# Extra TensorE products of ones in the routing of a Macaron layer (MoE, Mamba, MoE)

## What is computed

```
x = x + 0.5 * moe(layernorm(x))
x = x + mamba(layernorm(x))
x = x + 0.5 * moe(layernorm(x))
```

```
logits = xf @ gate_w + gate_b                 # 4096 x 64 experts
top_l, top_i = top_k(logits, 3)
gates = softmax(top_l)
pos = (cumsum(onehot) * onehot).sum(-1) - 1   # place of each choice in its expert
valid = pos < 64
buf[e, pos] = xf[tok]                         # then two matrix products per expert with a GELU between
```

## Time and profile before

| | |
|---|---|
| Median of 3 runs | 862.25 us (859.62 to 864.14) |
| Profiled execution | 867.32 us, its span 865.6 us |
| TensorE busy | 683.7 us (79%) |
| VectorE busy | 623.0 us (72%) |
| GpSimd busy | 462.6 us (53%) |
| ScalarE busy | 419.1 us (48%) |
| Mean granted TensorE clock | 0.886 |

### The profile page before, as it was taken

How to read it: one execution, slowest core, us unless ns; L and a number is a source line. 1 busy time by engine, 2 the same in 40 slices (tenths; PEclk the granted TensorE clock), 3 DMA queues, 4 the chain that set the end, 5 groups by cost and what they waited for, 6 DMA issues and landing times. The chain is left out here.

```text
span 865.6 us, 27705 instructions
## 1 busy us (share of the span) xinstructions
PE 683.7 (79%) x11818; PEld 426.1 (49%) x11818; DVE 623.0 (72%) x1053; ACT 419.1 (48%) x779; POOL 462.6 (53%) x301
## 2 busy tenths in 40 slices
PE   5637999956456889899798989978886537999967
PEld 3625555545123445446454644545453525555546
DVE  7782555529246989899998989898996891555525
ACT  2410544420457867758676766756531320444520
POOL 3003666420013878798787778878992003566520
PEclk9857999979558999999999999989996757999979
DMA  8992999443055363443425353442004901999537
GB/s 289 396 322 74 341 378 300 160 153 153 5 167 182 120 201 103 140 153 111 154 92 183 111 155 137 114 153 97 3 4 158 396 29 47 329 379 308 181 112 295
DMA packets 92100, 155.47 MB, mean 180 GB/s; under 512 B 7315, under 2 KB 32541, under 8 KB 90704
## 3 DMA queue, kind: packets, MB, share of 16 engines
q1 hardware_dynamic: 87568, 141.40, 48.0%
q0 software_dynamic: 4416, 12.39, 4.1%
HBM read 112.02 MB, written 41.99 MB: 178 GB/s over the span
## 5 line engine op out<-in xcount | busy, mean ns | idle before, releaser
L1143 POOL TENSOR_TENSOR BIG<-BIG,R 128x1024 f32<-128x1024 f32 x128 | 301.1, 2372 | 65.5 <-DVE BIG L1097 65.4
L1097 DVE TENSOR_TENSOR_SCAN BIG<-BIG,ps 128x1024 f32<-128x1024 f32 x128 | 286.0, 2271 | 4.2 <-PE ps L849 2.9
L849 PE MATMUL ps<-BIG,stack 64*32 64x128 f32 x8192 | 154.1, 282 | 48.6 <-DVE BIG L1097 46.8
L849 PEld LDWEIGHTS ps<-BIG,stack 64*32 64x32 f32 x8192 | 118.9, 108 | 125.4 <-DVE BIG L1097 100.7
L1019 ACT ACTIVATE BIG<-BIG,An 128x510 f32<-128x510 f32 x192 | 124.0, 708 | 10.2 <-DVE BIG L1097 9.7
L717 POOL DMA_INDIRECT R<-xn_dram,tok_idx x64 | 65.2, 1019 | 100.7 <-DVE row_idx L645 80.9
L731 POOL DMA_INDIRECT y_dram<-BIG,row_idx x64 | 64.6, 1010 | 69.0 <-DVE BIG L669 63.3
L654 DVE COPY BIG<-ps 128x512 f32<-128x512 f32 x64 | 44.3, 692 | 74.1 <-PE ps L501 74.1
L390 ACT ACTIVATE BIG<-BIG 128x512 f32<-128x512 f32 x64 | 40.4, 631 | 104.9 <-DVE BIG L661 104.9
L871 PE MATMUL ps<-BIG,fold 128*32 128x512 f32 x512 | 70.1, 623 | 5.0 <-POOL BIG L1143 5.0
L501 PE MATMUL ps<-BIG 128*64 128x512 f32 x240 | 68.6, 651 | 0.0
(11 more groups left out here) (153 smaller groups left out, 972.4 us busy)
## 6 DMA issues: line engine op xcount, KB each, us to landing
BIG<-in_L_ffn_w SPq DMA_DIRECT2D x120, 512.0 KB, 6.3
dt_dram<-state_more SPq DMA_DIRECT2D x16, 1024.0 KB, 4.3
BIG<-dt_dram SPq DMA_DIRECT2D x48, 256.0 KB
BIG<-y_dram SPq DMA_DIRECT2D x18, 512.0 KB, 9.2
R<-c_dram SPq DMA_DIRECT2D x32, 256.0 KB
y_dram<-zeros SPq DMA_DIRECT2D x3, 2048.0 KB, 17.3
y_dram<-zeros SPq DMA_DIRECT2D x6, 1024.0 KB, 9.7
xn_dram<-R POOLq DMA_DIRECT2D x2, 2048.0 KB, 11.0
```

The lines of the kernel that those rows point to most:

```text
L849: last = nc.tensor.matmul(ps[CW * slot:CW * slot + CW, 2 * (st % 2) + b, :] .rearrange("p (g s k) -> p k g s", g=2, k=4)[:, k], dT[q % 2][ ...
L1097: nc.vector.tensor_tensor_scan(state[st % 3], dA[:, st % 6].rearrange("p b g t -> p (b g t)"), ps[:, u:u + 2, :].rearrange("p b n -> p (b ...
L1143: nc.gpsimd.tensor_tensor(prod[st % RP], state[st % 3].rearrange("p (b g t) -> p b g t", b=2, g=2), Cf[q % 2][:, 2 * gp:2 * gp + 2].rearra ...
```

## The change

A helper `keep_clock(bank, count)` issues `count` bf16 products of the matrix of ones with 512 columns of ones into a PSUM bank; nothing reads them. It is called with bank 5 at four places: ten products ahead of the wait for the gate bias (f = 0 alone), twelve behind the bias products, eleven ahead of the code products, fourteen behind them. In front of the eleven stand new waits: for the second count of `picked`, and with f = 0 for ScalarE's copies out of bank 5.

```diff
+            def keep_clock(bank, count):
+                for _ in range(count):
+                    nc.tensor.matmul(ps[:, bank, :], ones[:, :], ones[:, :].unsqueeze(1).broadcast_to([P, 4, P]),
+                                     start=True, stop=True)
+
             if f == 0:
                 e.wait_ge(G("ones"), 3)
+                keep_clock(5, 10)
                 e.wait_ge(G("gwb"), 32)
             else:
                 e.wait_ge(M("scanned"), STEPS * NQ)
...
                 nc.tensor.matmul(L[:, tiles(g)[0]:tiles(g)[0] + n, :], one[:, :],
                                  gb[:, :].unsqueeze(1).broadcast_to([1, n, E]), start=True, stop=False)
+            keep_clock(5, 12)
             if f == 1:
                 e.wait_ge(M("x"), NQ)
             ln_transpose(e, LS, 0)
...
             last.then_inc(S("before"), 1)
 
+            if f == 0:
+                e.wait_ge(G("bias"), HC)
+                e.wait_ge(G("vcol"), C2)
+                e.wait_ge(G("A"), 1)
+            e.wait_ge(*S.at("picked", 2))
+            keep_clock(5, 11)
             for k in range(K):
                 e.wait_ge(*S.at("WL", k + 1))
                 e.wait_ge(*S.at("WH", k + 1))
...
             last.then_inc(S("code"), 1)
+            keep_clock(5, 14)
```

## The result

The changed kernel takes 855.02 us in the median of 20 runs (850.65 to 859.83), the kernel before 863.35 us (859.62 to 871.1, 20 runs). The ratio is 0.9908, 95% interval 0.9886 to 0.9929: 7.9 us faster by the ratio, 8.3 us by the medians. The forecast was 5.3 us faster and 857.0 us, with a range of 850.5 to 862. The profiled execution has a span of 852.8 us (865.6 before) and a mean clock of 0.904 (0.886 before).

A forecast was written before the change was run, and what follows sets the result against it. TensorE's low clock in the two serial routings was taken to slow logits and first expert pairs. 2.5 + 1.6 - 1.0 + 2.2 = 5.3 us saved, 862.0 against the profiled execution, 857.0 against the runs; range 850.5 to 862.

The forecast's parts named there:

- signs of being wrong: First routing's first transpose after 21 us, code products faster, or experts' first L501 still 1.97 us in both routings.
- Part 3: Eleven products ahead of the code products: no faster code products, 0.5 us lost each routing, 1.0 in all; bounds 0 and 1.6.
- Part 1: Ten products ahead of the first routing's bias: 4.2 us at most, to 8.9 us, costing nothing, making room for the twelve.
- Part 2, first routing: Twelve products between bias and transposes: 2.5 us saved taken; ends 4.7 saved and 5.0 lost.
- middle case: First routing: twelve end near 19 to 20, transposes 3 us late, logits group 1 near 25; 2 to 3 us saved.
- best end: First routing: bias ends at 13.4, the twelve at 15.9, logits group 1 at 24 instead of 27.2; 4.7 us saved.
- (d): All parts at their best ends, 4.7 + 2.4 + 4.2: 11.3 us saved, 851.0; chance 0.10 including near it.
- Second routing: Twelve products between bias and transposes: at most 0.2 us late, up to 2.4 us saved, 1.6 taken.
- Part 4: Fourteen products behind the code products: faster experts' start, 2.1 us each routing halved to 1.1, 2.2 in all; bounds 0 and 4.2.
- (a): Same time: the clock comes up and falls again in the gaps; 0.5 us saved, 861.7; chance 0.17.
- (b): Same time: transposes don't hold the clock, so the twelve's high clock is lost before the first logits; 861.0; chance 0.11.
- (c): Slower: 1.2 GHz from bias through first logits, first transposes at 21.6 instead of 16.60; 4.9 us lost, 867.2; chance 0.07.

The follow-up runs named there:

- one-row control: Changed kernel with every extra product reading one row of ones instead of 128; 1.0064 of the kernel before, 5.6 us slower.
- parts 1 and 2 alone: Changed kernel with only the ten products ahead of the bias and the twelve behind it; 0.9992 of the kernel before.
- part 4 alone: Changed kernel with only the fourteen products behind the code products; 0.9952 of the kernel before, about 4.2 us faster.

## Why the prediction was right, and where not

**Sign and mechanism** were right, and the time was inside the range: 7.9 us against 5.3, and the one-row control shows that it is the clock. Of the signs that the prediction named, L501 at 1.1 us and the second routing's wait (0.42 us) came true; the first routing's wait was 1.56 us and not under 1. One of its signs of being wrong came true as well: the code products got faster (Part 3 below). That the sum was near is in part luck, errors of both signs: part 3 cost less than taken, part 4 gave more, and the runs with parts 1 and 2 alone show less of them than was taken.

**Part 1** was right: 4.42 us, ended at 9.2, before the bias landed at 10.02, and its use is only the room it makes. Whether this room matters, its removal only suggests.

**Part 2, first routing.** The middle case came nearly to the letter: the clock fell in the bias, the twelve ended at 19.3, group 1 of the logits stood at 25.1. The best end was added up wrong: with group 1 at 24 instead of 27.2, VectorE saves 3.2 us there and its second wait of 0.91, some 4.1 us and not 4.7, and (d) comes to 10.7 us saved; only the low end of the range hangs on it. It gave 3.46 us in this profile for 2.5 taken, and 1.75 in the second profile of the same kernel. **Second routing:** 2.81 and 1.54 us for 1.6 taken, the first above the bound of 2.4, which counted group 1 alone. The statement that at most 0.2 us is late failed in three of five profiles, where the bias products ran at 1.2 GHz throughout and the transposes began 2.8 us late. Those are profiles; the timed runs of the variants show less for parts 1 and 2 together, 0.7 us alone and 1.5 us beside part 4 (0.9952 against 0.9935), each within some 3 us, for 4.1 taken. It is the term with the largest scatter.

**Part 3** failed in one step, the cost of 0.5 us for each late start of the code products: the start was late by 0.9 us, near the 0.7 forecast, but the code products won it back, and B changed by minus 0.1 and plus 0.4 us instead of plus 0.5 each; over twelve routings 0.1 us was paid of 0.7 in the mean. The observation beneath it, that the clock does not pace these products, held. I had taken their spacing as fixed at 64 ns and not asked what sets it; it came down to 55 ns, and what sets it is still open. Its upper bound of 1.6 us is more than the two times 0.7 that the text gives for it.

**Part 4** is the term that was mis-sized: 2.36 and 2.79 us in the profile, 4.2 us in the timed runs of part 4 alone, for 2.2 taken with 4.2 as bound. Halving was the step, though the 18 routings above speak for some of it (1.6 us each in the mean, 3.2 in all): I read the fall 1.1 us after the code products as the time that the clock outlasts work, and the code products turn out to be poor at holding it (it fell amid them at 61.0 with TensorE busy throughout), while fourteen products of 512 columns held it over 1.6 us of idle time. It does not do so every time. The bound left out the first L511, which the trace of before has at 1.06 us instead of 0.75, and the third pair, whose L501 in the second routing took 1.42 us.

**The rivals.** (a) gave 861.7 and (b) 861.0 us, some 6 us above the measured median. (b)'s mechanism is refuted for the mixed stretch: once up at 20.05, the clock held through all transposes and logits, sixteen products in 1.98 us. The rule that the prediction cites from the Trainium skill, TensorE: Matmul & The Clock Gate, Part 4: PE-mode transpose, is about transposes alone, and no stretch of those is long enough here. (c) is what the one-row kernel brings about: first transposes 5.5 and 3.4 us late and at 1.2 GHz, 5.6 us slower; priced at 4.9.

**What stays open:** how the gain divides between parts 1 and 2 and part 4. Part 4 alone is worth 0.5%; the rest adds 0.3% beside it and 0.1% alone, with intervals that overlap. Why the clock falls within the code products, or just behind the fourteen, in some routings and not in others was not tried, nor what makes the code products faster.

## What to carry to other kernels

Extra products pay where an engine's wait covers them and TensorE work that others wait for follows at once: behind the last product before a wait for a DMA, not in front of work that others wait for. In front of such work they can be paid in full (eleven more ahead of the code products: 8.4 us), so compare their time with the wait that they shorten. Fewer can do as well: 21 per routing gave 0.9931 and 47 and 37 gave 0.9922. A stretch that is paced by something else than the array, as the code products of 64 columns here, gains nothing from a high clock.

## What the runs showed of the hardware

- Being busy is not enough for the clock. It fell during unbroken bias products of one row (13.2 us; in the earlier trace rows as they ended, at 664.15), during unbroken 64-column products at 2.4 GHz (61.0 us), and stayed low under 5.3 us of one-row bf16 products of 512 columns, where among or just behind the same with 128 rows it rose.
- One bf16 product of 128 rows and 512 columns takes 0.42 us at 1.2 GHz and, from the fourteen in 3.19 us, 0.23 us or a little less at 2.4 GHz.
- Executions of one kernel differ in when the clock rises: stretch A of the changed kernel was 18.92 and 20.63 us in two profiles, D was 7.8 to 10.7 us among profiles with the same fourteen products. A single profile of such a change can be off by several microseconds, and 12 runs leave 0.3%.
- The 192 products of 64 columns took 12.34 us at either clock in the kernel before and down to 10.89 us behind extra products, with starts 55 ns apart. The clock level does not explain it, and the first microsecond being the slowest speaks against a head start.
- The page's clock of 1.0 at the start of an execution can stand for 1.2 GHz; the durations tell.
